# Last phase of a transformer layer kernel: which engine sums the expert rows, and which adds the residual

## What is computed

```python
x = x + _layernorm(_L0_attn_ref(_layernorm(x, axis=-1), ...), axis=-1)
x = x + _layernorm(_L0_ffn_ref(_layernorm(x, axis=-1), ...), axis=-1)
return x
```

```python
y = jnp.sum(yk * topk_w[..., None].astype(yk.dtype), axis=1)
shared = jax.nn.silu(x @ Sg.T) * (x @ Su.T) @ Sd.T
return (y + shared).reshape(B, S, H)
```

## Time and profile before

| | us |
|---|---|
| median of 3 runs (lowest, highest) | 1404.93 (1403.07, 1407.63) |
| the profiled execution's own time | 1400.53 |
| span of the profiled execution | 1398.8 |
| mean granted clock of TensorE, as a share of full speed | 0.964 |
| busy: PE, DVE, ACT, POOL | 1232.7, 875.7, 832.7, 925.7 |

### The profile page before, as it was taken

How to read it: one execution, slowest core, us unless ns; L and a number is a source line. 1 busy time by engine, 2 the same in 40 slices (tenths; PEclk the granted TensorE clock), 3 DMA queues, 4 the chain that set the end, 5 groups by cost and what they waited for, 6 DMA issues and landing times.

```text
span 1398.8 us, 25701 instructions
## 1 busy us (share of the span) xinstructions
PE 1232.7 (88%) x7872; PEld 857.2 (61%) x7872; DVE 875.7 (63%) x2413; ACT 832.7 (60%) x2256; POOL 925.7 (66%) x1112
## 2 busy tenths in 40 slices
PE   3589999899999989989989998999966999999984
PEld 1356556576666666656666665666633677778953
DVE  5677657678668767867876876786666322222237
ACT  2476558677777777767677776777744332323413
POOL 3577646468886976878788697788855513444554
PEclk9899999999999999999999999999987999999977
DMA  6467697645655454444435444454434559898683
GB/s 201 101 164 166 168 240 151 167 82 119 128 108 103 85 106 94 83 95 80 93 72 91 91 78 80 82 80 85 80 87 139 162 151 238 224 233 215 133 247 121
DMA packets 364489, 182.70 MB, mean 131 GB/s; under 512 B 287248, under 2 KB 343030, under 8 KB 364352
## 3 DMA queue, kind: packets, MB, share of 16 engines
q1 hardware_dynamic: 344768, 166.18, 51.4%
q0 software_dynamic: 16416, 11.70, 4.7%
q10 hardware_dynamic: 3168, 3.15, 0.7%
HBM read 75.32 MB, written 64.69 MB: 100 GB/s over the span
## 4 chain that ended last, share of the span: by engine, by line
PE 34%; DVE 16%; POOL 16%; DMA 13%; ACT 11%; issue 10%; SPq 0%; ACTq 0%; POOLq 0%; DVEq 0%
DMA Y<-W,wix 7%; PE bank L927 6%; POOL PH L864 5%; POOL P L859 5%; DMA PT<-PH 5%; PE bank L956 5%; ACT P L1186 4%; PE bank L971 4%; POOL BUF L626 4%; PE bank L1033 3%; PE bank L942 3%; PE bank L1090 3%; PE bank L988 2%; PE bank L1049 2%; PE bank L1103 2%
## 5 line engine op out<-in xcount | busy, mean ns | idle before, releaser
L864 POOL TENSOR_TENSOR PH<-P,PH 128x512 f16<-128x512 f32 x256 | 300.3, 1173 | 169.8 <-ACT PH L1195 167.1
L927 PE MATMUL bank<-RB,W 128*128 128x512 f16 x1092 | 282.0, 384 | 17.1 <-DVE RB L377 14.0
L956 PE MATMUL bank<-RB 128*128 128x256 f32 x1024 | 252.2, 388 | 33.7 <-DVE RB L1299 13.1
L859 POOL TENSOR_SCALAR P<-P,rr 128x256 f32<-128x256 f32 x512 | 247.7, 492 | 47.3 <-DVE rr L1320 47.3
L1186 ACT ACTIVATE P<-bank,nm 128x256 f32<-128x256 f32 x512 | 237.9, 475 | 26.2 <-DVE nm L1324 19.1
L626 POOL DMA_INDIRECT BUF<-RT,ix x192 | 201.7, 1051 | 67.9 <-issue 35.7
L971 PE MATMUL bank<-PT,RB 128*128 128x256 f16 x1536 | 213.9, 276 | 33.7 <-DVE O L1330 24.6
L956 PEld LDWEIGHTS bank<-RB 128*128 128x128 f32 x1024 | 184.6, 191 | 70.8 <-issue 22.9
L1195 ACT ACTIVATE PH<-P 128x512 f16<-128x512 f32 x256 | 163.4, 638 | 91.1 <-POOL P L859 52.6
L971 PEld LDWEIGHTS bank<-PT,RB 128*128 128x128 f16 x1536 | 147.2, 99 | 107.8 <-issue 46.1
L1178 ACT ACTIVATE O<-bank,bqk 128x256 f16<-128x256 f32 x256 | 123.2, 481 | 125.0 <-PE bank L971 124.9
(11 more groups left out here) (200 smaller groups left out, 1675.0 us busy)
## 6 DMA issues: line engine op xcount, KB each, us to landing
RB<-in_ewT SPq DMA_DIRECT2D x24, 352.0 KB
BUF<-zrow SPq DMA_DIRECT2D x4, 1926.0 KB, 8.8
W<-BUF SPq DMA_DIRECT2D x64, 120.4 KB, 4.1
HT<-in_ewT SPq DMA_DIRECT2D x18, 352.0 KB
HT<-in_wc SPq DMA_DIRECT2D x24, 256.0 KB, 3.6
HT<-in_ws SPq DMA_DIRECT2D x24, 256.0 KB, 4.1
Y<-zrow SPq DMA_DIRECT2D x10, 512.0 KB, 3.1
RB<-in_ewd SPq DMA_DIRECT2D x24, 176.0 KB
```

The lines of the kernel that those rows point to most:

```text
L859: r = eng.tensor_scalar(p, p, rr[:, w % 4, t:t + 1], SP_, ALU.mult, ALU.mult)
L864: eng.tensor_tensor(PH[:, w % 2, 1, :], P[:, w % 2, :], PH[:, w % 2, 0, :], ALU.subtract).then_inc(s["pl"], 1)
L927: r = eng.matmul(bk_[:, :], W[:, m, a, c * 2048 + h * 128:c * 2048 + (h + 1) * 128], XT[:, bp % 2, b, c, :], start=(k == 0), stop=(k == n ...
L956: r = eng.matmul(bS[u % 2][:, t * 256:(t + 1) * 256], QK[:, i % 2, 0, q * 256 + t * 128:q * 256 + (t + 1) * 128], QK[:, i % 2, 1, q * 256: ...
```

## The change

TensorE now adds both parts of groups 0 and 1 itself (`PE_SUM = 2`): 8 matmuls for such a group instead of 4, with a wait for the group's loads instead of a wait for Pool. Pool's `s0` and `s1` are gone. Pool now adds both halves of the residual for groups 0 to 5 (`DVE_X1 = 6`), and VectorE adds its half for groups 6 and 7 only. Pool's order is a new string.

```diff
-POOL_LAST = "s0 s1 s2 s3 x0 s4 x1 s5 x2 x3 s6 s7 x4 x5 x6 x7"
+POOL_LAST = "s2 s3 s4 x0 x1 s5 s6 x2 s7 x3 x4 x5 x6 x7"
+PE_SUM = 2
+DVE_X1 = 6
...
             def last_x1(g):
                 f = fin[g]
-                eng.wait_ge(s["fn"], 2 * g + 1)
                 if g < 4:
                     eng.wait_ge(s["xr"], 64)
                 else:
                     eng.wait_ge(s["po"], PO_END)
-                eng.tensor_tensor(half(f[:, 0], 0), half(f[:, 0], 0), half(x1[g], 0), ALU.add).then_inc(s["fx"], 1)
+                for h in range(2 if g < DVE_X1 else 1):
+                    eng.wait_ge(s["fn"], 2 * g + h + 1)
+                    r = eng.tensor_tensor(half(f[:, 0], h), half(f[:, 0], h), half(x1[g], h), ALU.add)
+                r.then_inc(s["fx"], 1)
...
             def last_add(g):
-                eng.wait_ge(s["fa"], g + 1)
+                if g < PE_SUM:
+                    eng.wait_ge(s_fl[g], 32)
+                else:
+                    eng.wait_ge(s["fa"], g - PE_SUM + 1)
+                parts = (0, 1) if g < PE_SUM else (0,)
                 for t in range(4):
-                    r = eng.matmul(LB_[g % 4][t // 2][:, t % 2 * 256:(t % 2 + 1) * 256], ident[:, :],
-                                   fin[g][:, 0, t, :], start=False, stop=(t % 2 == 1), skip_group_check=True)
+                    for k in parts:
+                        r = eng.matmul(LB_[g % 4][t // 2][:, t % 2 * 256:(t % 2 + 1) * 256], ident[:, :],
+                                       fin[g][:, k, t, :], start=False, stop=(t % 2 == 1 and k == parts[-1]),
+                                       skip_group_check=True)
                 r.then_inc(s["fp"], 1)
...
             for n, gs in enumerate(BATCH):
                 last_stats(gs)
-                if n:
-                    for g in BATCH[n - 1]:
+                for g in BATCH[n - 1] if n else ():
+                    if g >= DVE_X1:
                         last_x1(g)
             for g in BATCH[-1]:
                 last_x1(g)
```

More of the change, by code:

```diff
@@ L821, in _ @@
                 eng.wait_ge(s["fx"], g + 1)
-                eng.wait_ge(s["fy"], g + 1)
+                if g >= DVE_X1:
+                    eng.wait_ge(s["fy"], g - DVE_X1 + 1)
                 eng.dma_start(out[g * 512:(g + 1) * 512, :].rearrange("(t p) d -> p t d", p=128), fin[g][:, 0, :, :]
@@ L1419, in last_x1 @@
                 eng.wait_ge(s["fn"], 2 * g + 2)
-                if g < 4:
-                    eng.wait_ge(s["xr"], 64)
                 eng.tensor_tensor(half(f[:, 0], 1), half(f[:, 0], 1), half(x1[g], 1), ALU.add).then_inc(s["fy"], 1)
```

## The result

The changed kernel took 1408.99 us in the median of 15 runs, the kernel before 1404.47 us in 15 runs beside it: a ratio of 1.0043, with a 95% interval of 1.0026 to 1.0059. It is slower, by 0.43% or about 6 us, with an interval from 3.7 to 8.3 us; the two medians shown differ by less, 4.5 us. The change was forecast at +5.5 us, with a time of 1410.5.

The account below looks back on a forecast made before the run. Bound: when group 1 is summed in PSUM, and VectorE's time from batch to batch. 3.84 + 2.04 - 0.83 + 1.24 - 0.74 = +5.55 us, on 1404.93 gives 1410.5; range 1405 to 1414.5.

Parts of the forecast that it names:

- TensorE's term: Ahead of the first batch's statistics, 16 more matmul records at 0.24 us each delay ScalarE's first start by 3.84 us.
- the second distance: Time between ScalarE's second and third batch starts: 9.91 us forecast against 10.74 before, -0.83.
- the signs that the prediction named: Wrong if ScalarE's first distance stays under 10.5 us, its first start moves under 2, or VectorE idles before later BN_STATS.
- The first batch's small steps meet no Pool work: Ahead of ScalarE's first start, s4 can start at 1355.2 and is over by 1357.7; steps begin at about 1358.8.
- The count of waiting steps: Between ScalarE's starts, one small step passes per Pool addition (1.23 us): distances 11.97, 9.91, 7.65, 4.59 us.
- The check on before: The same count applied to the first distance of the kernel before: 9.91 us counted, 9.93 measured.
- Rival 1: In the last phase VectorE keeps its 10 slow steps and only removed additions count: +0.2 us, 1405.1; chance 0.12.
- rival 3: Only Pool's sums, not its residual additions, stall VectorE's small steps: -2.3 us, 1402.6; chance 0.05.
- rival 4: TensorE too late for groups 6 and 7: +6 to +9 us, 1411 to 1414; chance 0.09.
- group 5, which I had in time: TensorE's matmuls for group 5 were to be done at 1371.7, needed at 1373.2.
- rival 2: TensorE's clock is already full when its additions begin, its term 1.5 instead of 3.84: +3.2 us, 1408.1; chance 0.06.
- the 1.7 us of the forecast: Pool's part: six additions off VectorE's path (3.6 us), given back as small steps waiting for Pool, +1.7 us in all.

Follow-up runs that it names:

- TensorE's part alone: Kernel before, with TensorE summing both parts of groups 0 and 1, the residual still added half by Pool, half by VectorE: ratio 1.0035.
- Pool's part alone: Kernel before, with Pool adding both residual halves of groups 0 to 5 and summing all groups itself, in the changed kernel's order: ratio 1.0008.

## Why the prediction was right

**The sign and the size.** +0.43% was measured, +0.39% forecast. The last phase of the changed kernel run again is 6.1 us longer than that of before; the forecast's 5.55 is made of the same parts, and three of them were off. Part of the agreement is luck: in the changed kernel run again TensorE's term came out 0.4 us smaller than forecast and the second distance 0.7 us larger, and the ratio's own interval is 3.7 to 8.3 us. By the signs that the prediction named, one came true against it: VectorE was idle ahead of BN_STATS in the third batch, for 3.6 us, in both traces.

**TensorE's term, 3.84 us.** Measured 3.4 at the start of the phase, in TensorE's part alone and in the changed kernel run again. The clock turned at the same place in both as before, about 5 us after the additions began, as forecast. What was off is the price of a record. I took 1.92/8 = 0.24 us from a run of eight overflow records, which holds about 0.2 us at the changes from one kind of matmul to the other. In an unbroken run the additions start each 0.216 us (eight of them from 1352.21 to 1353.94 in the trace of before), and 16 x 0.216 = 3.5. In the first trace of the changed kernel the overflow matmuls took 1.0 us more (13.99) and the clock turned 2 to 3 us after the additions began, which together give 3.2.

**"The first batch's small steps meet no Pool work."** This step failed in the traced execution: s4 cost the steps 2.1 us of waiting. I had put s4's start at 1355.2, three us behind s3's, but Pool did not wait for group 4's loads in the kernel before, so no row showed when they land. In the eight traces in which Pool did, s4 started 18.5 to 18.9 us after the first load was issued; in the trace of before that is 1356.1 to 1356.5, over by 1358.6 to 1359.0, with the steps at 1358.8. So there never was a margin. Besides, loads and steps are set by two chains (Pool's last scatter, TensorE's clock) that shift against each other by up to 2.7 us from trace to trace. In the second trace of the changed kernel s4 ended just as the steps began.

**The count of waiting steps.** Right to 0.1 us for every distance in which TensorE was in time: 12.05, 9.99, 7.72, 4.66 in the kernel with 128 rows against 11.97, 9.91, 7.65, 4.59. The check on before that stood ahead of it, and the run with cut additions behind it, make this the best supported part. The one step of 3.76 us in the changed kernel with 2 small steps is the exception to it. Rival 1 (waits do not grow) and rival 3 (only sums stall) are out: steps wait beside sums and residual additions alike.

**TensorE's lateness (rival 4).** Priced at 0 and held at 0.09 as a case of its own; it was there in both traces of the changed kernel, but small: the second distance is 10.6 instead of 9.9. I had tried the half clock on group 6 alone; it was groups 4 and 5 that ran at it (four runs of eight records at 3.71 us), so group 5, which I had in time, was late. As I had said, part of the lateness fell into time in which steps would have waited for Pool: in the third batch two steps waited instead of five.

**The clock (rival 2).** The clock did not become full ahead of the additions on its own. Made full by 128 rows, it did not help the time either. The rival's price had assumed that TensorE's earliness reaches ScalarE; in the trace Pool's sums stood in between.

**Adding up.** TensorE's part alone +0.35%, Pool's part alone in the same order +0.08%, both +0.43 to 0.46%. That the parts add is what the times say, taken on two chips; the traces' sums do not add (4.4 and 5.2 us for the parts, 6.1 and 8.1 for both). Since the interval of Pool's part holds both 0 and the 1.7 us of the forecast, its size in the median stays open.

## What to carry to other kernels

- Before work is handed from VectorE to GpSimd, look for chains of very small VectorE operations beside it: a 128x512 addition that costs VectorE 0.6 us costs a chain 1 us in waiting if it meets one, and nothing if it meets statistics work. In the traces shortening the chain (12 steps to 2) was worth 6.8 us of the last phase, more than any division of the additions tried here; the times alone did not settle it.
- Where several engines feed one another closely, a gain on one is taken by the next: read the start of each batch from one engine's timeline and ask what now runs beside the small operations.
- One profiled execution fixes mechanisms and distances well and offsets between chains badly. A margin of a microsecond between two chains is no cover, least of all when one end of it is extrapolated.
- Take the price of a record from a long run of the same kind: a short run of another kind made 16 records 0.4 us too dear.

## What the runs showed of the hardware

- While GpSimd runs two-input additions back to back, one small VectorE step gets through per addition: 1.19 us a step beside 128x512, 0.65 us beside 128x256. One step in the traces here waited through three additions instead (3.76 us). BN_STATS of four tiles takes 1.42 us with Pool at work (from 1379.16 before) and 1.43 with Pool idle (from 1372.16 without the residual). With two steps per batch VectorE's own 128x512 additions met Pool's too, and there both engines were held: 1.75 us instead of 0.68 on VectorE, and a Pool addition of 1.80 instead of 1.26. The rows are from the kernel before with 2 small steps:

```profile
1364.99 1.75 DVE L1427 TENSOR_TENSOR RB<-RB,SSf 128x512 f32<-128x512 f32 x1
```

```profile
1364.40 1.80 POOL L898 TENSOR_TENSOR RB<-RB,SSf 128x512 f32<-128x512 f32 x1
```

- TensorE was busy for 13 to 14 us with the 64-row overflow matmuls at a granted clock of 0.50 in each trace. With 128 rows, half of them zero, the same 32 records took 8.8 us in the changed kernel, with the clock at 0.92 from 1333 to 1336 and then 1.00, and 10.0 and 10.1 us in the two other kernels that had the edit.
- A record of the additions (128 rows) follows the one before it after 0.216 us at full clock and 0.43 us at half.
- Group 2's data came later when TensorE did the first sums: Pool's sum of it starts 11.6 us after the first load is issued in the kernel before (1349.19 - 1337.57), and after 11.6 to 11.8 us in all six traces in which Pool sums all groups; in the seven in which TensorE does the first sums it is 12.5 (1357.78 - 1345.26, the changed kernel) to 12.9 us. Group 4 starts after 18.5 to 18.9 us in both kinds. The loads and their rate are the same. I did not find the cause.
